# The mixer's output added in DRAM by a transfer of GpSimd, with another order of the prologue

## The reference

```
h = layernorm(x) * (1 + ca) + sa
omega, zeta, F = softplus(h Wo + bo), sigmoid(h Wz + bz), h Wb + bb      # 64, 64 and 128 wide
scan over the 2048 rows: an oscillator of 64 (z, y) pairs, driven by F -> xs
x = x + ga * (xs C^T + h D^T)
h = layernorm(x) * (1 + cb) + sb
xr, xk = mu * h + (1 - mu) * (h of the row before)
x = x + gb * sigmoid(xr Wr) * (relu(xk Wk)^2 Wv)
```

## Time and profile before

| | |
|---|---|
| median of three executions | 980.42 us |
| the profiled execution | 980.24 us, its span 978.4 us |
| TensorE matmuls | 937.1 us busy, 96% |
| VectorE | 817.8 us, 84% |
| ScalarE | 696.8 us, 71% |
| GpSimd | 91.4 us, 9% |
| TensorE's granted clock | 0.983 of full in the mean |

### The profile page before, as it was taken

The page is one execution under the profiler, slowest core; times in us unless marked ns, Lnnn a source line. Parts: engine busy times, 40 slices in busy tenths (PEclk is TensorE's granted clock), DMA queues, the critical chain, the costliest instruction groups (busy, mean ns, idle before and its releaser), DMA issues.

```text
span 978.4 us, 14767 instructions
## 1 busy us (share of the span) xinstructions
PE 937.1 (96%) x5019; PEld 786.4 (80%) x5020; DVE 817.8 (84%) x2270; ACT 696.8 (71%) x1371; POOL 91.4 (9%) x117
## 2 busy tenths in 40 slices
PE   9977968899999999999999999999999999998997
PEld 3566857788888888888888888888888888887886
DVE  4878759798898979898997989898997988697562
ACT  4979776778868686877768676886768677765451
POOL 0001001000200101110110201110020101000000
PEclk9999988899999999999999999999999999999999
DMA  9820302021221311021131302021131301111001
GB/s 328 279 76 1 108 3 84 1 88 42 72 70 44 99 44 65 23 86 44 44 97 44 97 22 88 21 87 44 44 97 44 97 7 38 44 44 44 22 22 44
DMA packets 35275, 64.78 MB, mean 66 GB/s; under 512 B 3704, under 2 KB 4344, under 8 KB 35200
## 3 DMA queue, kind: packets, MB, share of 16 engines
q1 hardware_dynamic: 35200, 63.84, 19.5%
HBM read 47.02 MB, written 16.81 MB: 65 GB/s over the span
## 4 chain that ended last, share of the span: by engine, by line
PE 84%; ACT 7%; DVE 6%; issue 1%; DMA 1%; SPq 0%; POOL 0%; DVEq 0%; ACTq 0%; POOLq 0%
PE ps_kr L328 32%; PE ps_cd L328 20%; PE ps_tv L328 18%; PE ps_pt L328 7%; PE ps_pt L336 3%; PE ps_tv L369 2%; ACT mix_full L725 1%; PE ps_tv L389 1%; ACT square_out L584 1%; DVE mix_full L977 1%; DMA x<-in_wmod 1%; PE ps_kr L389 1%; DVE tmp L1198 1%; ACT x_in L602 1%; ACT x_in L574 1%
## 5 line engine op out<-in xcount | busy, mean ns | idle before, releaser
L977 DVE SCALAR_TENSOR_TENSOR mix_full<-ps_tv,cur_m,mix_full 128x256 f32<-128x256 f32 x256 | 119.0, 479 | 42.3 <-ACT mix_full L725 42.2
L747 ACT ACTIVATE kk<-ps_kr 128x512 f32<-128x512 f32 x64 | 38.2, 598 | 124.7 <-PE ps_kr L328 124.4
L725 ACT ACTIVATE mix_full<-ps_tv,cur_m 128x255 f32<-128x255 f32 x256 | 120.1, 573 | 6.3 <-PE ps_tv L369 6.3
L1468 POOL TENSOR_SCALAR var<-sq 128x2 f32<-128x2 f32 (+1 forms) x35 | 34.4, 982 | 680.7 <-ACT square_out L584 680.7
L328 PE MATMUL ps_kr<-mix_k_hi,wk_hi 128*128 128x256 f32 x512 | 80.7, 280 | 5.6 <-issue 5.5
L328 PE MATMUL ps_kr<-mix_k_lo,wk_hi 128*128 128x256 f32 x512 | 80.0, 279 | 0.0
L328 PE MATMUL ps_kr<-mix_k_hi,wk_lo 128*128 128x256 f32 x512 | 79.7, 278 | 0.0
L328 PEld LDWEIGHTS ps_kr<-mix_k_hi,wk_hi 128*128 128x128 f32 x512 | 70.9, 190 | 8.9 <-issue 6.5
L328 PE MATMUL ps_tv<-wv_hi,kk_hi 128*128 128x512 f32 x256 | 72.0, 404 | 1.2 <-issue 1.2
L328 PE MATMUL ps_kr<-wr_hi,mix_r_hi 128*128 128x512 f32 x256 | 70.6, 398 | 2.1 <-ACT kk L747 2.1
L328 PE MATMUL ps_tv<-wv_lo,kk_hi 128*128 128x512 f32 x256 | 69.7, 394 | 0.0
(11 more groups left out here) (215 smaller groups left out, 2246.5 us busy)
## 6 DMA issues: line engine op xcount, KB each, us to landing
x<-in_x SPq DMA_DIRECT2D x32, 512.0 KB, 3.7
out<-x SPq DMA_DIRECT2D x32, 512.0 KB, 2.8
x_in<-in_x SPq DMA_DIRECT2D x15, 1024.0 KB, 5.2
x<-in_wmod SPq DMA_DIRECT2D x3, 1024.0 KB, 7.7
mix_full<-in_wmod SPq DMA_DIRECT2D x2, 1024.0 KB, 9.0
x_in<-in_x SPq DMA_DIRECT2D x2, 512.0 KB, 5.7
stage_out<-in_wd SPq DMA_DIRECT2D x1, 1024.0 KB, 10.0
stage_mix<-in_wmod SPq DMA_DIRECT2D x1, 1024.0 KB, 10.5
```

Source lines behind the costliest of these rows:

```text
L725: mm = act.activation(mix[n][:, k, 1:UNIT], ps_tv[:, j, c * UNIT:(c + 1) * UNIT - 1], ACT.Identity, bias=cur_m[:, SHIFT + k:SHIFT + k + 1] ...
L747: act.activation(kk[:, i, :], ps_kr[:, i, :], ACT.Relu).then_inc(s_relu, 1)
L977: dve.scalar_tensor_tensor(mix[n][:, k, :], ps_tv[:, j, c * UNIT:(c + 1) * UNIT], cur_m[:, alpha + k:alpha + k + 1], mix[n][:, k, :], ALU. ...
L1468: pool.tensor_scalar(var[:, :], sq[:, :], 1.0 / D, EPS, ALU.mult, ALU.add).then_inc(s_var, 1)
```

## The change

The mixer's product rt is no longer added to x2 by VectorE. SP stores x2, the x before the mixer, as soon as residual is done, and a transfer on GpSimd's queue adds rt to the same rows of out in DRAM (accum_op=add). It waits for that plain store and for read_out(u). tanh(u) waits for the adding transfer of unit u - 1 to land. SP's load of unit u + 3 waits for the plain store of unit u - 1 and for normalise2 of that unit. The prologue's order changes on TensorE, ScalarE, VectorE and GpSimd; in it the statistics of chunk 3 move from ScalarE (sums1(3), squares1(3)) to VectorE (statistics1(3)), and one warming group of matmuls goes. The diff, with renamed semaphores and the split of projections_out into omega_out and zeta_and_b_out cut to their core:

More of the change, by code:

```diff
@@ L203, in build @@
         s_rvg = sem("s_rvg")
-        s_out = sem("s_out")
-        s_stored = sem("s_stored")
+        s_added = sem("s_added")
+        s_stored = [sem(f"s_stored{r}") for r in range(4)]
         x_rows = d["x"].rearrange("(q i p) n -> q p i n", p=P, i=TPC)
@@ L308, in _ @@
                     sp.dma_start(x_in[:, :, :], x_rows[q]).then_inc(s_xin, 16)
-                sp.wait_ge(s_out, u * TPU + 2 * TPU)
-                sp.dma_start(out_units[u], x2[:, u % 4]).then_inc(s_stored, 16)
+                sp.wait_ge(s_x2, u * TPU + TPU)
+                sp.dma_start(out_units[u], x2[:, u % 4]).then_inc(s_stored[u % 4], 16)
                 if s + 1 == UPB and b + 1 < B:
+                    sp.wait_ge(s_rvg, u * TPU + TPU)
                     sp.dma_start(gate_b[:, :], rows[1, b + 1:b + 2, :].partition_broadcast(P)).then_inc(s_gate_b, 16)
-            sp.wait_ge(s_stored, 16 * (NUNIT + 1))
+            for r in range(4):
+                sp.wait_ge(s_stored[r], 16 * (NUNIT // 4))
         @block.tensor
@@ L468, in k_product @@
                 if u == 0:
-                    pe.wait_ge(s_weight_lo["wk"], 1)
+                    pe.wait_ge(s_weight_lo["wk"], 2)
                 for m in range(KC):
@@ L646, in angles_first, with omega_out @@
                 act.activation(om_exp[:, :], om_exp[:, :], ACT.Ln, bias=1.0).then_inc(s_softln, 1)
-            def projections_out(q):
-                if q:
-                    act.wait_ge(s_rec, (q - 1) * STEPS + STEP_RECIPROCAL)
-                halves = [(slice(n * M, n * M + M), slice(n * HALF, (n + 1) * HALF)) for n in range(2)]
-                lower, upper = slice(0, M), slice(M, 2 * M)
+            lower, upper = slice(0, M), slice(M, 2 * M)
+            halves = [(slice(n * M, n * M + M), slice(n * HALF, (n + 1) * HALF)) for n in range(2)]
+            def omega_out(q):
+                act.wait_ge(s_rec, (q - 1) * STEPS + STEP_RECIPROCAL)
                 act.wait_ge(s_p, q * 2 + 1)
@@ L658, in projections_out, with zeta_and_b_out @@
                     act.activation(om_exp[to, :], ps_pt[lower, 0, cols], ACT.Abs, bias=scan_bias[lower, 0:1])
+            def zeta_and_b_out(q):
+                for to, cols in halves:
                     act.activation(ze[to, :], ps_pt[upper, 0, cols], ACT.Exp, bias=scan_bias[upper, 1:2])
                 act.wait_ge(s_p, q * 2 + 2)
+                if q == 1:
+                    act.wait_ge(s_cols["cb"], 1)
                 for to, cols in halves:
@@ L666, in projections_out @@
                 mm.then_inc(s_pev, 1)
+            def projections_out(q):
+                omega_out(q)
+                zeta_and_b_out(q)
             def softplus_parts(q):
@@ L1012, in statistics1 @@
                 dve.wait_ge(s_norm_bias1, q)
-                done = (q - 3) * TPC
+                done = (q - 2) * TPC
                 for i in range(TPC):
@@ L1300, in _, with half_low @@
             dve.tensor_tensor(silu_c[:, :, :], silu_c[:, :, :], c_in[:, :, :], ALU.mult).then_inc(s_silu, 1)
+            def half_low(what, half):
+                dve.wait_ge(s_weight_hi[what], 1)
+                (hi, lo), k = WEIGHTS[what], slice(2 * half, 2 * half + 2)
+                low(lo[:, k, :], STAGE[what][:, k, :], hi[:, k, :], s_weight_lo[what])
             def weight_low(what):
@@ L1440, in _ @@
                         new_columns(b + 1, tab_h, cur_h, s_cur_h)
-                    beside(rec, add_out(u - 1), 2)
+                    take(rec, 4)
                     if next_mix:
@@ L1472, in rstd1_of @@
             def rstd1_of(q):
-                if 1 <= q <= 3:
+                if 1 <= q <= 2:
                     rstd_of(sq1, var1, rstd1, q, s_sq1, s_var1, s_rstd1)
```

9 lines of the change are left out of this document (4 added, 5 removed).

## The result

Five executions of each on one chip: 989.26 us in the median (987.25 to 989.63) against 982.46 (979.67 to 983.04) of the kernel before, ratio 1.0073 with a 95% interval of 1.0057 to 1.009. The change makes the kernel slower, by 0.7%. The forecast was 984.7 in 978.5 to 990.5: the right side and inside the range, 4.6 us short. The profiled execution took 989.26 us, its span is 987.5 against 978.4.

The account below looks back on a forecast made before the run. TensorE was taken as the bound, busy 200.00 of every 200 us from 200 to 800, so only prologue and end count. (D - 1.9) + (D - 4.0), with D = 5.2, gives +4.5 on 980.24: 984.7 us, range 978.5 to 990.5.

Parts of the forecast that it names:

- part 7: From t1_first_half(3) to unit 4's states: mixes(2) 4.15 us later by the same steps, VectorE regaining 0.85, states +3.3 us.
- narrower forecast: Whole kernel: D from 4 to 6.5 us gives 982.3 to 987.3 us, chance 0.50.
- D: Price of one adding transfer, from read_out's end to its semaphore: taken as 5.2 us, between 2.8 and 8.4.
- Parts 1 and 3: Steady part: removing 38 us of VectorE adds gains nothing; tanh's wait for the transfer costs 0, with 15.1 us of room.
- Part 4: Prologue to v_product(0): k_product(0) 8.6 us earlier, this early lead lost in ScalarE's queue, v_product(0) at 96.0, +0.65 us.
- Part 6: Prologue: tanh(1) waits for add_out(0), queued behind rstd1_of(3); t1_first_half(3) at 133.0 + D, 138.2, +4.15 us.
- Short add: Both places where the transfer lies open: GpSimd's queue as quick as SP's, D 3.2 us, total 980.7 us; chance 0.18.
- The lead that survives: ScalarE's queue between 53 and 70: up to 5.75 us of charged waits vanish, total 979.0 us; chance 0.15.
- Long add: Adding transfer long or its issue held up by VectorE: D 8.4 us, total 991.1 us; chance 0.12.
- The order is neutral: Whole kernel: nothing that matters is unloaded and tanh(1) doesn't wait, total 980.2 us; chance 0.05.

Follow-up runs that it names:

- experiment 5: Kernel before with its old prologue, sums as adding transfers, unit 0's issued ahead of rstd1_of(3): 983.74 us, ratio 1.0026 to the kernel before.
- experiment 8: New prologue order with VectorE's sums, one plain store per unit, no adding transfer, h_high(3, (0, 1)) behind mix_high(2, 0): 975.57 us, ratio 0.9937 to the kernel before.
- experiment 11: Kernel of experiment 7 with chunk 2's statistics on VectorE instead of ScalarE and k_low(0) ahead of mixes(1): 974.03 us, ratio 0.9931 to the kernel before.
- experiment 1: Changed kernel with add_out(0) ahead of rstd1_of(3) in GpSimd's list: 979.67 us, ratio 0.9985 to the kernel before.
- experiment 2: Changed kernel with ScalarE's h_high(3, (0, 1)) back behind mix_high(2, 0): 985.75 us, ratio 1.0044 to the kernel before.
- experiment 10: Changed kernel with 38 matmuls on constants on TensorE during its wait before t1_first_half(3): 986.58 us, ratio 1.0056 to the kernel before.
- experiment 9: Changed kernel with GpSimd's transfer plain instead of adding, so out lacks x: 982.81 us, ratio 1.0018 to the kernel before.
- experiment 12: Kernel of experiment 7 with 25 matmuls on constants on TensorE during its wait before t1_first_half(2): 974.25 us, ratio 0.9929 to the kernel before.
- experiment 7: Changed kernel with add_out(0) ahead of rstd1_of(3), h_high(3, (0, 1)) behind mix_high(2, 0), last unit's sum on VectorE: 973.65 us, ratio 0.9921 to the kernel before.
- experiment 3: Changed kernel with both add_out(0) ahead of rstd1_of(3) and h_high(3, (0, 1)) behind mix_high(2, 0): 976.21 us, ratio 0.9946 to the kernel before.

## Why the prediction was right, and where it fell short

**Right in its mechanisms.** Of the span's +9.1 the prediction had +4.5; of the medians' +6.8, +4.3. The missing 4.6 us of span are 0.6 at t1_first_half(3), 3.3 from there to unit 4's states (part 7) and 1.3 at the end, less 0.6 in TensorE's stretch between, which no part forecast. So the range was met, but the narrower forecast of 982.3 to 987.3 was missed though D lay in its bounds.

- Parts 1 and 3, the sums taken off VectorE are worth nothing in the steady part: shown by the stages and by experiment 5. The plain stores land in 5.6 us in place of 2.8; in the steady part SP issues them right behind a load (550.21 and 550.63), where it issued them apart as a rule before (583.88, the next load at 586.70). SP's loads wait for them 26 times, and unit 1's adding transfer once (to 158.63), but no matmul waits for these. tanh waits for an adding transfer once in the whole run, at unit 1. Part 1 has one exception: in the prologue, once nothing else holds mixes(2), the sums of unit 1 are worth 1.5 us at the states (experiment 8).
- Part 4: k_product(0) at 68.75 (68.9 forecast), normalise1(2) at 91.60 (91.5), ScalarE's three idles 1.43, 1.76 and 2.57 us (1.55, 1.6, 2.6), v_product(0) at 96.21 (96.0). The early lead did go in ScalarE's queue; experiment 11 shows VectorE as the next bound behind it.
- Part 6: tanh(1) waited for the adding transfer behind rstd1_of(3), and experiment 1 shows that this was the largest part of the loss. t1_first_half(3) at 138.81 (138.2) is nearer than its terms deserve: recurrence(1) ended 1.2 us later than forecast and D was 1.2 longer, while the table load stood in front of the wait (124.08), not behind it, which saved 1.3, and the 0.6 of handovers added by rounding up didn't come. That misses cancelled there is luck. Unit 0's transfer could not have gone at 107 either, but from 113, when its plain store had landed; with the queue order as it was, that cost nothing.

**The step that failed: part 7**, "mixes(2) comes by the same steps, 4.15 later". It came 8.65 later (153.29 in place of 144.64). The diff moves h_high(3, (0, 1)) in front of shifted(2); I costed the move at nothing. It waits for states_part(3), and the 2.8 us that shifted(2) lost by it went straight to k_product(2); experiment 2 measures 3.1 at the states. The other 1.1 is TensorE's lower clock, which lasted longer than before (experiment 10 shows what it costs, none why it lasts). VectorE regained 1.47 us of it before the states, where 0.85 was forecast; the two steps that this came from are 0.80 by the prediction's own numbers.

**Mis-sized terms.** D was 5.2 and measured 6.4 in the prologue and 6.5 at the end (7.0 less 0.5): +1.2 and +1.3, and the end cost 2.5 in place of 1.2. That the addition costs something above a plain transfer was right; it is 2.7 us (experiment 9), and how much of that is the read of DRAM stays open. By the Trainium skill, DMA: Bandwidth & Descriptors, section "Anatomy of one DMA — SWDGE (gpsimd) path", a transfer of GpSimd's queue of this size takes 3.2 us (estimate from the page). The trace agrees for the plain one, 3.4, and not for the adding one, 6.1. By the Trainium skill, the same page, section "SWDGE vs HWDGE vs iDMA", VectorE's two-port modes lock GpSimd out of the state that its descriptors are written to. No run here shows it: the issue took 1.40 us at 126.62 and 1.21 at 981.10 with VectorE idle, and 1.27 in the median of all 32, and from issue to tanh(1) the first took 6.07 us, against a median of 6.1 to land. The other term too small was the lower clock behind t1_first_half(2): v_product(0) takes 7.2 us where it took 5.6, and recurrence(1) ends 2.7 us later, where 1.6 was forecast. At full clock (experiment 12) recurrence(1) ends 1.1 us earlier (120.27 against 121.33 in experiment 7).

**The rivals.** Short add: refuted (D 6.4 against its 3.2); even the plain transfer of experiment 9 has 3.7. The lead that survives: refuted by the 96.21. Long add, 8.4: refuted in both places that count; the longest of the 32 took 10.0 us to land, and nothing waited for it. The order is neutral: refuted, and in an unexpected way, since with two lines moved it is 5.4 us better than the old one at the states (experiment 3).

What stays open: why TensorE's stretch behind the states varies by 2 us from kernel to kernel, what sets how long the lower clock lasts behind t1_first_half(3), and whether the adding transfer is worth anything against VectorE's sum (0 to 2 us, experiments 7 and 8).

## What to carry to other kernels

When a diff reorders a queue, list for each moved instruction what it waits for and what now stands behind it. One instruction that must wait makes all behind it wait, however ready they are, and two such moves here (GpSimd's transfer, ScalarE's h_high) cost 12.6 us, 2.5 of it through TensorE's clock, and hid a gain of 5.4. A transfer in place of an engine's sum is free only where something covers its whole way from issue to landing, so give the last one, which nothing covers, back to the engine. And a wait on TensorE costs more than its length when the lower clock follows. Filling one such wait won 1.9 us here (experiment 10); filling another won 1.0, which was gone again at the next stretch at the lower clock (experiment 12), so measure it at the end and not behind the wait.
